# The least busy expert of a routed feed-forward stage in four column groups of 32 tokens

## Reference

```python
def _L1_ffn_ref(x, gate_w, routing_bias, w1, w2, w3, sw1, sw2, sw3):
    E = 16
    K = 4
    def _swiglu(x, w1, w2, w3):
        a = x @ w1
        return a * jax.nn.sigmoid(a) * (x @ w2) @ w3
    gate_out = x @ gate_w + routing_bias
    top_v, top_i = jax.lax.top_k(gate_out, K)
    chosen = jax.nn.one_hot(top_i, E, dtype=x.dtype).sum(axis=-2)
    masked = jnp.where(chosen > 0, gate_out, NEG)
    probs = jax.nn.softmax(masked, axis=-1)
    weights = probs * chosen
    out = _swiglu(x, sw1, sw2, sw3)
    for e in range(E):
        out = out + _swiglu(x, w1[e], w2[e], w3[e]) * weights[..., e:e + 1]
    return out

xn = _layernorm(x, axis=-1)
x = x + _L0_gnn_ref(...) + _L0_mix_ref(...)
x = x + _L0_ffn_ref(_layernorm(x, axis=-1)[None], ...)[0]
xn = _layernorm(x, axis=-1)
x = x + _L1_gnn_ref(...) + _L1_mix_ref(...)[0]
x = x + _L1_ffn_ref(_layernorm(x, axis=-1)[None], ...)[0]
```

## Time and profile before

| | us |
|---|---|
| median of 3 runs | 493.23 (491.24 to 493.54) |
| the profiled execution, in all | 493.42 |
| its span in the profile | 491.3 |
| TensorE busy | 478.7 (97% of the span) |
| VectorE, ScalarE, GpSimd busy | 251.3, 190.4, 7.9 |
| DMA | 191.57 MB, 390 GB/s on average |

### The profile page before, as it was taken

One profiled execution on the slowest core, in us unless ns is written; L12 is line 12 of the kernel. 1 busy time (PEld: TensorE's weight loads), 2 busy tenths in 40 slices (PEclk: granted clock), 3 DMA queues, 4 the chain that ended last, 5 costly groups with the idle time before them and its releaser, 6 DMA issues.

```text
span 491.3 us, 6674 instructions
## 1 busy us (share of the span) xinstructions
PE 478.7 (97%) x2592; PEld 300.1 (61%) x2592; DVE 251.3 (51%) x324; ACT 190.4 (39%) x216; POOL 7.9 (2%) x47
## 2 busy tenths in 40 slices
PE   7989799999999999999999999999999999999997
PEld 4747433436775775666666667566666666756534
DVE  6734440126787164744655484475465548447012
ACT  1110100025855266425545453553554546244000
POOL 2000000001000000000000000000000000000000
PEclk9988899999999999999999999999999999999999
DMA  8999999999939979999999999999999999999980
GB/s 331 421 420 422 422 421 418 422 415 410 400 147 414 363 287 418 396 406 417 417 415 413 416 417 414 415 413 419 416 415 412 417 415 411 414 415 414 418 328 32
DMA packets 37043, 191.57 MB, mean 390 GB/s; under 512 B 4090, under 2 KB 4474, under 8 KB 31636
## 3 DMA queue, kind: packets, MB, share of 16 engines
q1 hardware_dynamic: 36816, 191.01, 95.6%
q10 hardware_dynamic: 196, 0.14, 0.1%
HBM read 190.87 MB, written 0.26 MB: 389 GB/s over the span
## 4 chain that ended last, share of the span: by engine, by line
PE 94%; DVE 3%; ACT 1%; DMA 1%; issue 1%; POOL 0%; DVEq 0%; POOLq 0%
PE ps L1737 17%; PE ps L1715 17%; PE ps L1800 13%; PE ps L1815 9%; PE ps L1722 8%; PE ps L1365 4%; PE ps L1529 3%; PE ps L1781 2%; PE ps L1558 2%; PE ps L1546 1%; PE ps L1358 1%; PE ps L1820 1%; PE ps L1427 1%; PE ps L1785 1%; PE ps L1964 1%; PE ps L1417 1%
## 5 line engine op out<-in xcount | busy, mean ns | idle before, releaser
L973 DVE TENSOR_TENSOR s_lo<-w_raw,s_hi 128x1365 fp32r<-128x1365 f32 x64 | 98.9, 1577 | 32.3 <-ACT s_hi L715 30.8
L715 ACT CAST s_hi<-w_raw 128x1365 fp32r<-128x1365 f32 x64 | 83.5, 1335 | 17.1 <-DMA w_raw<-in_w 14.4
L1737 PE MATMUL ps<-w_raw,exS 128*64 128x512 f32 (+1 forms) x544 | 83.7, 455 | 0.0
L1715 PE MATMUL ps<-s_hi,xT_hi 128*128 128x512 f32 (+1 forms) x192 | 78.1, 407 | 0.6 <-DVE s_lo L973 0.6
L1715 PE MATMUL ps<-s_lo,xT_hi 128*128 128x512 f32 (+1 forms) x192 | 70.4, 369 | 0.0
L1737 PEld LDWEIGHTS ps<-w_raw,exS 128*64 128x64 f32 x544 | 36.9, 137 | 45.9 <-issue 45.7
L728 ACT CAST s_hi<-w_raw 128x1536 fp32r<-128x1536 f32 (+1 forms) x32 | 43.6, 1370 | 39.5 <-DMA w_raw<-in_w 39.5
L987 DVE TENSOR_TENSOR s_lo<-w_raw,s_hi 128x1536 fp32r<-128x1536 f32 (+1 forms) x32 | 51.1, 1614 | 0.0
L1722 PE MATMUL ps<-s_hi,xT_lo 128*128 128x512 f32 (+1 forms) x192 | 50.4, 370 | 0.0
L1815 PE MATMUL ps<-w_raw,hTS 128*64 128x512 f32 (+1 forms) x176 | 44.5, 601 | 0.0
L1715 PEld LDWEIGHTS ps<-s_hi,xT_hi 128*128 128x128 f32 x192 | 36.1, 188 | 13.2 <-issue 5.1
(11 more groups left out here) (313 smaller groups left out, 483.0 us busy)
## 6 DMA issues: line engine op xcount, KB each, us to landing
w_raw<-in_w SPq DMA_DIRECT2D x128, 682.5 KB, 8.5
w_set<-in_w SPq DMA_DIRECT2D x31, 1024.0 KB, 23.7
w_raw<-in_w3s SPq DMA_DIRECT2D x27, 768.0 KB, 9.4
w_raw<-in_w SPq DMA_DIRECT2D x24, 768.0 KB, 7.8
w_raw<-in_sw SPq DMA_DIRECT2D x8, 682.5 KB, 15.3
w_raw<-in_w3s SPq DMA_DIRECT2D x9, 512.0 KB, 11.4
w_raw<-in_w SPq DMA_DIRECT2D x8, 512.0 KB, 8.4
wk_sb<-in_wk SPq DMA_DIRECT2D x2, 1024.0 KB, 16.1
```

The costliest lines, as they stand in the source:

```text
L715: a.copy(s_hi[pair_of(g)][:, 0:F1], raw[:, 0:F1]).then_inc(hi_ready, 1)
L973: v.tensor_tensor(s_lo[pair][:, 0:F1], raw[:, 0:F1], s_hi[pair][:, 0:F1].bitcast(F32), ALU.subtract).then_inc(lo_ready, 1)
L1715: mm(bank(i + c0 // D)[:, 0:n], xT_hi[:, k], w[:, c0:c0 + n], start=(k == 0 and w is s_hi[pair_of(g)]), stop=False)
L1737: last = mm(bank(NC * part + c0 // D)[FEW * g:FEW * g + FEW, 0:n], exS[:, k, tokens], w[:, CW * g + c0:CW * g + c0 + n], start=(k == 0), s ...
```

## The change

The last expert gets a form of its own. With 16 experts and 4 choices of 128 tokens, the least busy one has at most 32 tokens. So it runs in four column groups of 32 tokens, each with a quarter of the columns (QW = 342). `up_least` takes the place of `up_few` and `up_last` for it: each step k of w1 and of w2 is four matmuls of 342 columns; the addition of the expert before comes after w2's second step. VectorE multiplies 342 columns in one instruction, TensorE transposes three tiles of 114 columns, ScalarE copies them once. The down product takes 12 tiles of 114 rows (four groups times three) instead of 11 of 128. For this w3 has a third layout, `w3q`, made on the host for all experts, of shape 16 x 114 x 12 x 512; the four loads of the last w3 read it: 114 rows of three tiles (6,144 B) each, into the place of `w3_raw` and of the tile behind it (`bout_all`, used long before). Of `spread`, the last expert's column block is made by four matmuls of 32 tokens instead of two of 64. Left out below are the declarations of arguments, semaphores and the helper `quarter`.

```diff
--- before
+++ after
@@ -46,6 +46,7 @@
 W3_UNITS = len(DOWN)
+LEAST_DOWN = [(3 * u, 3) for u in range(W3_UNITS)]
 FEW = P // 2
@@ -55,6 +56,12 @@
 S_HT = [(0, 4), (4, S_TILES - 4)]
+LEAST = P // 4
+QUARTERS = P // LEAST
+QW = HALVES * CW // QUARTERS
+Q_TILES = -(-QW // P)
+Q_ROWS = QW // Q_TILES
+assert Q_ROWS * Q_TILES == QW and E1 * (LEAST + 1) > P * K1
 BUSY = P * K1 // (FEW + 1)
...
@@ -147,8 +154,11 @@
     w2_raw = [c(f"w2_raw{k}", [P, HALVES * CW]) for k in range(KT)]
+    at_w3 = c.at
     w3_raw = c("w3_raw", [P, FT, D])
+    w3_least = place("w3_least", [P, Q_TILES * QUARTERS, D], F32, at_w3)
     bout_all = c("bout_all", [P, D])
+    assert Q_TILES * QUARTERS == FT + 1
     pair_at = [c.at, c.at + size_pair, at_tail, at_tail + size_pair, slot_at(3)]
@@ -333,6 +343,8 @@
 
+    least_rows = [ps[:, i, 0:QW] for i in (0, NC)]
+
     def poly_bank(k):
...
@@ -557,7 +572,11 @@
                 expert_then = expert_now
-            next_down(NE - 1, expert_then)
+            w = one_down(w3q, expert_then)
+            for u in range(W3_UNITS):
+                wait_unused(NE - 2, 2, u)
+                t0, n = LEAST_DOWN[u]
+                sp.dma_start(w3_least[0:Q_ROWS, t0:t0 + n], w[:, t0:t0 + n]).then_inc(ld_down[u], 16)
             for b in range(2):
@@ -852,9 +871,11 @@
                     copy_hTS(m - 1, 1)
-                    silu_few(m)
-            copy_hTS(NE - 1, 0)
-            copy_hTS(NE - 1, 1)
+                    act.wait_ge(raw_used, few_of[m, 0, KT - 1] + 1)
+                    act.wait_ge(h_ready, m)
+                    a.activation(act_a[:, 0:QW], least_rows[0], ACT.Silu).then_inc(act_ready, 1)
+            act.wait_ge(hT_ps, turned(NE - 1) + 1)
+            a.copy(hTS[0:Q_ROWS, 0:Q_TILES], tiles(NC + 1)[0:Q_ROWS, 0:Q_TILES]).then_inc(hTS_ready, 1)
 
@@ -1314,13 +1335,10 @@
             dve.wait_ge(act_ready, last + 1)
-            dve.wait_ge(first_cols_ps, 1)
+            dve.wait_ge(raw_used, few_of[last, 1, KT - 1] + 1)
             dve.wait_ge(hT_ps, turned(last))
             rows = hS[:].rearrange("p t n -> p (t n)")
-            v.tensor_tensor(rows[:, 0:D], act_a[:, 0:D], few_row(NC)[:, 0:D], ALU.mult).then_inc(h_ready, 1)
-            dve.wait_ge(raw_used, few_of[last, 1, KT - 1] + 1)
-            v.tensor_tensor(rows[:, D:S_OWN * P], act_a[:, D:S_OWN * P], few_row(NC)[:, D:S_OWN * P], ALU.mult)
-            gated_tails().then_inc(h_ready, 1)
+            v.tensor_tensor(rows[:, 0:QW], act_a[:, 0:QW], least_rows[1], ALU.mult).then_inc(h_ready, 1)
             for b in range(2):
@@ -1738,22 +1756,15 @@
 
-            def up_last(e):
-
-                tokens = slice(FEW * few_no(e), FEW * few_no(e) + FEW)
-                for c, (c0, n) in enumerate(S_CHUNK):
-                    for k in range(KT):
-                        if c == 0:
-                            pe.wait_ge(ld_up[1][k], 16 * (e + 1))
-                        for g in range(HALVES):
-                            last = mm(bank(NC + c)[FEW * g:FEW * g + FEW, 0:n], exS[:, k, tokens],
-                                      w2_raw[k][:, CW * g + c0:CW * g + c0 + n], start=(k == 0), stop=(k == KT - 1), skip_group_check=True)
-                        if c > 0:
-                            last.then_inc(raw_used, 1)
-                        elif k == 1:
-                            add_few(e - 1)
-                    if c == 0:
-                        last.then_inc(first_cols_ps, 1)
+            def up_least(e, part, k):
+
+                pe.wait_ge(ld_up[part][k], 16 * (e + 1))
+                w = (w1_raw, w2_raw)[part][k]
+                tokens = slice(FEW * few_no(e), FEW * few_no(e) + LEAST)
+                for g in range(QUARTERS):
+                    last = mm(least_rows[part][quarter(g)], exS[:, k, tokens], w[:, QW * g:QW * g + QW], start=(k == 0), stop=(k == KT - 1),
+                              skip_group_check=True)
+                last.then_inc(raw_used, 1)
 
@@ -1770,11 +1781,13 @@
                     up(unit_of[m, part, k], NC * part, k)
+                elif m == NE - 1:
+                    up_least(m, part, k)
                 else:
                     up_few(m, part, k)
 
             def transpose_h(e, c):
-                pe.wait_ge(h_ready, e + 1 + (c if e == NE - 1 else 0))
+                pe.wait_ge(h_ready, e + 1)
                 if is_full(e):
@@ -1881,6 +1894,11 @@
                 for q in range(n):
+                    if q0 + q == len(SPARSE) - 1:
+                        for g in range(QUARTERS):
+                            last = mm(rounds[KT + b][quarter(g), P * q:P * q + P], gates[:, q0 + q, 0:LEAST], ident[:], start=True, stop=True,
+                                      skip_group_check=True)
+                        continue
                     for g in range(HALVES):
@@ -1935,34 +1953,30 @@
                         spread_few(u - 1)
-                if m == NE - 1:
-                    h_taken(m - 1)
-                    up_last(m)
-                    break
                 for k in range(KT):
                     up_part(m, 1, k)
-                    if k == 2 and not is_full(m - 1):
+                    if k == (1 if m == NE - 1 else 2) and not is_full(m - 1):
                         add_few(m - 1)
                 if m == 1:
                     pe.wait_ge(round_ready, ROUNDS)
 
             last_e = NE - 1
-            for c in range(len(S_HT)):
-                transpose_h(last_e, c)
+            pe.wait_ge(h_ready, NE)
+            for t in range(Q_TILES):
+                last = t_.transpose(tiles(NC + 1)[0:Q_ROWS, t], hS[:].rearrange("p t n -> p (t n)")[:, Q_ROWS * t:Q_ROWS * t + Q_ROWS], ident[:])
+            last.then_inc(hT_ps, 1)
             pe.wait_ge(x3_ready, 1)
             for b in range(2):
-                for i in range(FT):
-                    t, g = i // HALVES, i % HALVES
+                for i in range(Q_TILES * QUARTERS):
+                    t, g = i // QUARTERS, i % QUARTERS
                     if b == 0:
                         if i % 3 == 0:
                             pe.wait_ge(ld_down[i // 3], 16 * (last_e + 1))
                         if i == 0:
                             pe.wait_ge(y_few_ready, few_no(last_e))
-                        if g == 0 and t in (0, KT):
-                            pe.wait_ge(hTS_ready, len(S_HT) * few_no(last_e) + t // KT + 1)
-                    own = own_rows(g) if t < S_OWN else slice(0, P)
-                    last = mm(last_halves[b][own], hTS[:, t, own], w3_raw[:, i, HALF[b]], start=(t == 0), stop=(t == S_OWN),
-                              skip_group_check=True)
+                            pe.wait_ge(hTS_ready, len(S_HT) * few_no(last_e) + 1)
+                    last = mm(last_halves[b][quarter(g)], hTS[0:Q_ROWS, t, quarter(g)], w3_least[0:Q_ROWS, i, HALF[b]],
+                              start=(t == 0), stop=(t == Q_TILES - 1), skip_group_check=True)
                 last.then_inc(last_ps, 1)
@@ -1986,7 +2000,8 @@
         few[:, FEW * g:FEW * g + S_TAIL, HALVES * S_OWN] = halves[:, g, S_OWN * P:]
-    return dense, few
+    least = full[1:, :QUARTERS * QW].reshape(E1, QUARTERS, Q_TILES, Q_ROWS, D).transpose(0, 3, 2, 1, 4)
+    return dense, few, least.reshape(E1, Q_ROWS, Q_TILES * QUARTERS, D)
 
```

More of the change, by code:

```diff
@@ L92, in gps_kernel @@
 def gps_kernel(nc, x, small_in, gcn_w, mlp_w, mlp_b, wq0, wk0, wv0, w1_0, b1_0, w2_0, b2_0,
-               gnn_w, gnn_b, wq1, wk1, wv1, wout, bout, w1, w2, sw1, sw2, w3, w3s, out):
+               gnn_w, gnn_b, wq1, wk1, wv1, wout, bout, w1, w2, sw1, sw2, w3, w3s, w3q, out):
     base = up32(nc.sbuf_base)
@@ L382, in gps_kernel @@
     x_hi_ready, x_lo_ready = sem("x_hi_ready"), sem("x_lo_ready")
-    negmax1_ready, exp1_ready, first_cols_ps = sem("negmax1_ready"), sem("exp1_ready"), sem("first_cols_ps")
+    negmax1_ready, exp1_ready = sem("negmax1_ready"), sem("exp1_ready")
     hi_ready, lo_ready, used, pads = sem("hi_ready"), sem("lo_ready"), sem("used"), sem("pads")
@@ L445, in own_rows, with quarter @@
         return slice(FEW * g, FEW * g + FEW)
+    def quarter(g):
+        return slice(LEAST * g, LEAST * g + LEAST)
     block = nc.Block()
@@ L1997, in laid_out @@
     w2_0 = i["L0_ffn_W2"].reshape(GROUPS, EG, CHUNKS0, KT, P, D).transpose(0, 2, 4, 3, 1, 5)
-    w3, w3s = down_rows(i["L1_ffn_sw3"], i["L1_ffn_w3"])
+    w3, w3s, w3q = down_rows(i["L1_ffn_sw3"], i["L1_ffn_w3"])
     small = [i[k].reshape(P, ET).view(np.float32) for k in ("src", "dst", "edge_weight")]
@@ L2013, in laid_out @@
         "w1": i["L1_ffn_w1"], "w2": i["L1_ffn_w2"], "sw1": i["L1_ffn_sw1"], "sw2": i["L1_ffn_sw2"],
-        "w3": w3, "w3s": w3s,
+        "w3": w3, "w3s": w3s, "w3q": w3q,
     }
```

## The result

The changed kernel took 497.18 us (median of 4 runs, 496.54 to 497.49), the kernel before 492.43 in the same comparison: 1.0109 of it, 95% interval 1.0095 to 1.0124. It is slower by 1.1%. The profiled execution took 497.29 us in all, with a span of 495.2.

What follows compares the result with a forecast made beforehand. TensorE was taken to set the end, with loads next. Last w3 landing 489.1 plus tail 8.3 gave end 497.4, +6.1 on 491.3; with 0.1 for the spread product, 499.6 on the profiled execution, 499.4 on the median; range 496 to 502.

Steps and rivals of the forecast that it cites:

- Six engines, 4.5 us a unit: Loads of the last w3: 114 rows go to 6 DMA engines, 4.5 us a unit for 1.7, last landing 489.1.
- Four column groups run side by side: Last expert's w1, w2 and down product: steps halve, two w1 steps 1.22 us; down product of the expert before 2.2 earlier.
- TensorE ready for w3: Before the last down product: TensorE would be ready for w3 at 477.2, 4.3 us sooner.
- The tail at 1.2 GHz: Behind the last w3 landing: idle TensorE drops to clock 0.50, so the tail costs 8.3 us, 5.8 at full clock.
- The stretch that the prediction took it from: Earlier idling in the profile before: TensorE busy 2.14 of 3.40 us, then clock 0.50 for 6.8 us.
- The rival with sixteen engines: Last w3 loads: 114 rows shared as 7 and 8, 1.9 us a unit at most; 486.1 us, 1.5% faster; chance 0.13.
- nothing lost: Last w3 loads, bound with 16 engines: shares of 7 and 8 rows would cost no load speed.

Runs made afterwards that it cites:

- the kernel with fillers: Three float32 matmuls with unused result put before the waits for the second, third and fourth unit of the last w3, on the changed kernel: 495.50 us, 1.0088 of before.

## Why the prediction was right

It said 499.4 us, 1.3% slower, within 496 to 502; measured are 497.18 us and 1.1%. Step by step, in spans and from the common point (457.14 for 458.57, so 1.43 us are taken off the predicted times):

- **Six engines, 4.5 us a unit.** Right: share 0.36 to 0.38, 6 small packets a load, landings 4.3 to 4.4 us apart, last landing 487.6, predicted 489.1 - 1.4 = 487.7. Shown by one number alone, the rows of the load: 114, 116 and 128 give 6, 4 and 16 engines and ends of 497, 509 and 487 us. This is what the Trainium skill says in "DMA: Bandwidth & Descriptors" (why a DMA increments its semaphore by 16): the largest divisor up to 16; the runs agree for 116, 117 and 120 rows too.
- **Four column groups run side by side.** Right: two w1 steps take 1.29 us for the predicted 1.22 (a record every 81 ns; the prediction's 71 ns does not go with its own 1.22 us for 16 records, which is 76 ns), the down product of the expert before starts 3.51 us earlier, 2.1 from the common point for 2.2. The last down product takes 1.93 us for 30 records at full clock, four steps of 0.48. Columns in quarters do what they were made to do.
- **TensorE ready for w3.** Predicted 477.2 - 1.4 = 475.8, measured 476.38: 0.6 late: the down product of the expert before takes 5.51 for 5.35 with the change to and from 32-column groups at its ends, each pair of steps 1.29 for 1.22, and what is left are hand-overs. This cost nothing, as the loads were late anyway; it would cost in the rival's case.
- **The tail at 1.2 GHz.** Right in cause, shown by the kernel with fillers; the size, 8.3 us, was 7.6 (495.2 - 487.6), for a step takes 0.9 and the clock came back with the final sum. The stretch that the prediction took it from does not decide it, though: from 30.6 to 34.0 us TensorE is busy 2.14 of 3.40 us in both traces, and the clock behind it was at 0.50 before and is at 1.00 here. That it fell in the tail was likely from one such case, not certain.
- **What remains of the difference**, 2.2 us between 499.4 and 497.18: 1.4 are the early stretch of low clock that the profile of before had and this one has not, and 0.7 the tail. That stretch probably also divides the runs of the kernel before, though only one of them has a trace: they are 491.24, 491.62, 493.23 and 493.54 us, and in the later comparisons its median is 491.34 to 491.74. Against these the change costs 5.4 to 5.8 us and not 4.75; the prediction, made on a run of 493.42, had 6.2.
- **The rival with sixteen engines** was priced at 486.1 us; the kernel that has them, with 128 rows, takes 486.67. That near hit hides two terms: its common point lies 1.2 us earlier (457.40 for 458.57), and the last unit landed near 479.3, some 2 us after the 477.2 that follows from the prediction's 478.1 to 478.6. With 112 rows on 16 engines, nearest to its words, it would have missed by 5 us (491.51), since "nothing lost" is not true of shares of seven rows: the records take 375 ns there, and the last unit lands at 480.93.

What stays open is why a record takes longer in those loads. A reading that fits most of them, not put to a run of its own: the Trainium skill, "SBUF — State Buffer" (Door 1: The DMA port swizzle), gives 16 ports, four rows to a port and the same port again 32 rows further, and "DMA: Bandwidth & Descriptors" (The descriptor swizzle) says that a load of 128 rows is shared so that each engine has one port to itself.
## What to carry to other kernels

Before a tile is cut to fit the arithmetic, look at what its row count does to the load: a prime factor such as 19 left 6 of 16 engines here, and padding 114 rows to 128 bought 10.5 us for 12% more bytes. A kernel in which engines and queues are both nearly full has little to give away on either side: the time that TensorE saved, some 3.7 us before the last product, went into a wait for a load that had ended 1.2 us ahead of its use. And when loads end last, put the work that needs the last one last, and no other behind it (1.2 us here between the medians, of which the trace bears out some 0.7; the two intervals overlap a little).

## What the runs showed that was not expected

- 15 or 16 engines can be busy and deliver 52 to 63%: 218 to 264 GB/s at a share of about 1, for 421, in loads of 64, 80 with 48, 112 and 120 rows. Even 15 engines with 8 rows each (491.98 us) are 6.5 us slower than 16 with 8 each (485.49), in kernels that differ in nothing else. Some 1.6 us of that, as an estimate, is TensorE's clock, 0.50 behind the waits: the 12 records behind the last landing and the sum take 1.93 + 1.89 us, where at full clock 24 such records took 1.92 us and the sum 1.25. With 117 rows the runs also spread widely, from 486.8 to 493.0 us.
- The low clock of the tail costs 1.7 us of 497, and 9 matmuls without any use win it back.
